# Local attention with two tiles per round instead of one

## The reference, cut to what matters

```python
bl = 128; nb = L // bl; G = L // 16          # L = 1024, H = 16 heads of 64
q = einsum('bld,dhk->blhk', x, Wq) / sqrt(64); k, v = ... Wk, Wv
side_k, side_v = (sum of x over 16 rows) @ Wk, Wv          # G = 64 rows
kb, vb = previous, own and next block of k, v              # 3 * 128 rows
logits = q_block @ concat(kb, side_k) + bias               # |distance| <= 127, else -1e9
m = max(logits.max(), 0)
probs = exp(logits - m) / (sum(exp(logits - m)) + exp(-m))
y = probs @ concat(vb, side_v)
x = x + einsum('blhk,hkd->bld', y, Wo)
```

## Time and profile before

| | us |
|---|---|
| median of three runs | 2113.58 |
| profiled execution | 2099.86 |
| its span (first to last instruction) | 2098.1 |
| PE matmul busy | 1908.6 (91%) |
| PE weight loads busy | 1372.2 (65%) |
| DVE busy | 1121.4 (53%) |
| ACT busy | 944.6 (45%) |
| POOL busy | 449.3 (21%) |

### The profile page before, as it was taken

One profiled execution on the slowest core, in us unless ns is written; L12 is line 12 of the kernel. 1 busy time (PEld: TensorE's weight loads), 2 busy tenths in 40 slices (PEclk: granted clock), 3 DMA queues, 4 the chain that ended last, 5 costly groups with the idle time before them and its releaser, 6 DMA issues.

```text
span 2098.1 us, 37599 instructions
## 1 busy us (share of the span) xinstructions
PE 1908.6 (91%) x15665; PEld 1372.2 (65%) x15665; DVE 1121.4 (53%) x2309; ACT 944.6 (45%) x1644; POOL 449.3 (21%) x502
## 2 busy tenths in 40 slices
PE   5888977995988949899999999999999999999998
PEld 3456965773656645667776776766777777777776
DVE  4474443016142126878887888854545543455544
ACT  2212022112242304778887888854454543445522
POOL 1352100004121033212121212112222222233313
PEclk8879567996998979999999999999999999999999
DMA  4000021112242339621100310000000000000001
GB/s 128 0 1 1 1 66 42 57 47 61 81 140 81 101 118 169 128 42 37 33 23 19 104 31 25 19 21 1 1 1 2 1 1 1 27 1 1 2 1 40
DMA packets 85194, 86.94 MB, mean 41 GB/s; under 512 B 34658, under 2 KB 70946, under 8 KB 84898
## 3 DMA queue, kind: packets, MB, share of 16 engines
q1 hardware_dynamic: 79154, 73.81, 13.2%
q0 software_dynamic: 3072, 8.39, 1.4%
q10 hardware_dynamic: 2800, 2.34, 0.4%
HBM read 65.65 MB, written 18.87 MB: 40 GB/s over the span
## 4 chain that ended last, share of the span: by engine, by line
PE 74%; DVE 18%; issue 3%; DMA 2%; POOL 1%; ACT 1%; SPq 0%; DVEq 0%; POOLq 0%
PE PS L1032 7%; DVE arena L1695 7%; PE PS L1024 7%; PE PS L1899 6%; PE PS L1883 6%; PE PS L1838 5%; PE PS L1528 5%; PE PS L1541 5%; PE PS L1873 5%; DVE arena L1700 4%; PE PS L519 3%; PE PS L1520 3%; PE PS L1843 3%; PE PS L1906 1%; PE PS L1933 1%
## 5 line engine op out<-in xcount | busy, mean ns | idle before, releaser
L1695 DVE CUSTOM_DVE_ANT_0 arena<-PS,arena 128x1024 f32<-128x1024 f32 x256 | 312.8, 1222 | 75.3 <-PE PS L1520 62.4
L1528 PE MATMUL PS<-arena 128*128 128x128 f32 x2048 | 281.8, 275 | 20.4 <-DVE arena L1700 20.2
L1619 ACT ACTIVATE arena<-arena 128x1024 f32<-128x1024 f32 x256 | 295.0, 1152 | 9.8 <-DVE arena L1695 9.8
L1528 PEld LDWEIGHTS PS<-arena 128*128 128x128 f32 x2048 | 241.4, 142 | 87.4 <-DVE arena L1700 34.8
L1980 ACT ACTIVATE arena<-arena 128x449 f32<-128x449 f32 (+1 forms) x256 | 162.5, 635 | 190.8 <-DVE arena L2014 190.8
L2069 POOL TENSOR_SCALAR arena<-arena 128x448 f32<-128x448 f32 (+1 forms) x256 | 154.3, 616 | 419.4 <-DVE arena L2005 419.4
L2014 DVE CUSTOM_DVE_ANT_0 arena<-PS,arena 128x448 f32<-128x448 f32 (+1 forms) x256 | 141.2, 590 | 138.9 <-PE PS L1874 138.0
L1615 ACT COPY arena<-PS 128x512 f32<-128x512 f32 x256 | 150.4, 588 | 102.9 <-PE PS L1528 94.7
L1700 DVE COPY arena<-PS 128x512 f32<-128x512 f32 x256 | 175.9, 687 | 1.2 <-PE PS L1528 1.2
L1024 PE MATMUL PS<-arena 128*128 128x512 f32 x384 | 170.2, 601 | 6.6 <-ACT arena L1123 6.6
L1032 PE MATMUL PS<-arena 128*128 128x256 f32 x768 | 172.2, 385 | 0.0
(11 more groups left out here) (279 smaller groups left out, 2657.0 us busy)
## 6 DMA issues: line engine op xcount, KB each, us to landing
arena<-in_L_ffn_W SPq DMA_DIRECT2D x16, 1024.0 KB, 6.6
arena<-prior SPq DMA_DIRECT2D x16, 512.0 KB, 4.0
parts<-arena SPq DMA_DIRECT2D x24, 256.0 KB, 5.4
arena<-parts SPq DMA_DIRECT2D x96, 64.0 KB, 2.9
arena<-parts SPq DMA_DIRECT2D x48, 128.0 KB, 10.5
ye<-arena SPq DMA_DIRECT2D x8, 512.0 KB, 3.5
prior<-arena SPq DMA_DIRECT2D x4, 1024.0 KB, 9.1
arena<-in_xT SPq DMA_DIRECT2D x2, 1024.0 KB, 8.0
```

The costliest lines, as they stand in the source:

```text
L1528: h = e.transpose(PS[:, i, P * j:P * j + P], Sb[z % 3][:, 512 * g + P * j:512 * g + P * j + P], ident)
L1619: e.activation(Sb[z % 3], Sb[z % 3], ACT.Exp, bias=mr[:, z % 4:z % 4 + 1], scale=-1.0).then_inc(s_exp, 1)
L1695: e.tensor_tensor_reduce(Sb[z % 3], ps, Ab[m % 2], 1.0, 3e38, ALU.add, ALU.min, mr[:, z % 4:z % 4 + 1]).then_inc(s_ttr, 1)
```

## The change

A round of every engine now takes two tiles, `z` and `z + 1` for even `z`. On PE:

- scores of `z` and `z + 1`; values of `z - 4` and `z - 3`; turn of `z - 2`, one piece of other work, turn of `z - 1`, another piece.
- The other work is listed by `between(z)`: chunks 0 and 1 in the first pair of a unit, 2 and 3 in the second, 4 in the third, 5 in the fourth. Projections come second in the third and fourth pairs (tiles 68, 70, 76, 78, 84, 86, 92 and 94).
- Values run two tiles behind the turn (one before).
- Scores have four banks (0 to 3), turned weights banks 4 and 5, values one bank (6), chunks and projections still bank 7. `Pb` has eight buffers. `Sb`, `Se` and `Pt` stay as they are.

ACT: `expo` of both tiles, then turn, chunk, turn, chunk. DVE: `biased` of both tiles, `recip(z)`, eviction of values, `recip(z + 1)`, then turn, work, turn, work. POOL's list stays.

```diff
-    Pb = [arena.up(512) for _ in range(6)]
+    Pb = [arena.up(512) for _ in range(8)]
...
-    N_ZERO = 13
-
-    def projected(z):
-        return (z - 66) // 2 if 65 < z < 82 and z % 2 == 0 else None
+    N_ZERO = 15
+    PRO = {z: t for t, z in enumerate(z for z in range(68, NZ, 2) if z % 8 in (4, 6))}
+    YB, CB = 6, 7
+    def between(z):
+        u, todo = z // 8 + 1, {0: (0, 1), 2: (2, 3), 4: (4,), 6: (5,)}[z % 8]
+        work = [(u, c) for c in todo] if u < NU else []
+        return work + ([("o", PRO[z])] if z in PRO and PRO[z] < TB_ else [])
...
         def scores(z):
-            w.wait_ge(*of(u).emptied((u, 5)))
+            w.wait_ge(*of(u).emptied((u, 1)))
...
-                w.wait_ge(s_ttr, x - 2)
+                w.wait_ge(s_ttr, x - 3)
...
         def values(z):
-            if t % 4 == 0:
-                w.wait_ge(s_y, n - 1)
+            w.wait_ge(*of(u).emptied((u, 5)))
+            w.wait_ge(s_y, n)
...
-        for z in range(NZ + 2):
-            if z < NZ:
-                scores(z)
-            if projected(z) is not None:
-                t = projected(z)
-                w.wait_ge(*ring.free(("o", t)))
-                project(0, t, ring.bank(("o", t))).then_inc(ring.sem, 1)
-            if 2 <= z:
-                values(z - 2)
-            if 1 <= z <= NZ:
-                turn(z - 1)
-            if z // 8 + 1 < NU and z % 8 < 6:
-                chunk(z // 8 + 1, z % 8)
+        for z in range(0, NZ + 4, 2):
+            for y in (z, z + 1):
+                if y < NZ:
+                    scores(y)
+            for y in (z - 4, z - 3):
+                if y >= 0:
+                    values(y)
+            work = between(z) if z < NZ else []
+            for y in (z - 2, z - 1):
+                if 0 <= y < NZ:
+                    turn(y)
+                if work:
+                    key = work.pop(0)
+                    if key[0] == "o":
+                        w.wait_ge(*ring.free(key))
+                        project(0, key[1], ring.bank(key)).then_inc(ring.sem, 1)
+                    else:
+                        chunk(*key)
...
     def act(e, w, own):
         def expo(z):
-                w.wait_ge(s_tf, x - 5)
+                w.wait_ge(s_tf, x - 7)
...
+        for z in range(0, NZ + 2, 2):
+            for y in (z, z + 1):
+                if y < NZ:
+                    expo(y)
+            work = between(z) if z < NZ else []
+            for y in (z - 2, z - 1):
+                if y >= 0:
+                    turn(y)
+                key = work.pop(0) if work else ("o",)
+                if key[0] != "o" and chunk_by(key[1]) == "act":
+                    chunk_out(e, w, *key)
...
     def dve(e, w, own):
+        for z in range(0, NZ + 4, 2):
+            for y in (z, z + 1):
+                if y < NZ:
+                    biased(y)
             if z < NZ:
-                biased(z)
...
+                recip(z)
+            for y in (z - 4, z - 3):
+                if y >= 0:
+                    values(y)
+            if z < NZ:
+                recip(z + 1)
+            work = between(z) if z < NZ else []
+            for y in (z - 2, z - 1):
+                if 0 <= y < NZ:
+                    turn(y)
+                if work:
+                    key = work.pop(0)
+                    if key[0] == "o":
+                        project(key[1])
+                    elif chunk_by(key[1]) == "dve":
+                        chunk_out(e, w, *key)
```

More of the change, by code:

```diff
@@ L1797, in phase_f @@
         first.plan(s, "dve" if s[0] == "sk" else "act")
-    for z in range(NZ):
-        if projected(z) is not None:
-            ring.plan(("o", projected(z)), "dve")
-        if z // 8 + 1 < NU and z % 8 < 6:
-            ring.plan((z // 8 + 1, z % 8), chunk_by(z % 8))
+    for z in range(0, NZ, 2):
+        for key in between(z):
+            ring.plan(key, "dve" if key[0] == "o" else chunk_by(key[1]))
     def f_steps(w):
@@ L1870, in scores @@
                 x, rows = 2 * z + d, slice(64 * d, 64 * d + 64)
-                w.wait_ge(s_ttr, x - 2)
+                w.wait_ge(s_ttr, x - 3)
                 q_ = q5[r][rows, P * t:P * t + P]
-                e.matmul(PS[:, x % 3, 0:nk], q_, k5[r][rows, P * k0:P * k1], start=True, stop=True)
-                e.matmul(PS[:, x % 3, nk:nk + 64], q_, sk[rows, u % 8, u // 8, :], start=True, stop=True).then_inc(s_sc, 1)
+                e.matmul(PS[:, x % 4, 0:nk], q_, k5[r][rows, P * k0:P * k1], start=True, stop=True)
+                e.matmul(PS[:, x % 4, nk:nk + 64], q_, sk[rows, u % 8, u // 8, :], start=True, stop=True).then_inc(s_sc, 1)
         def turn(z):
@@ L1882, in turn @@
                 for j in range(nj):
-                    h = e.transpose(PS[:, 3 + d, P * j:P * j + P], Pb[x % 6][:, P * j:P * j + P], ident)
+                    h = e.transpose(PS[:, 4 + d, P * j:P * j + P], Pb[x % 8][:, P * j:P * j + P], ident)
                 h.then_inc(s_tf, 1)
@@ L1898, in values @@
                     wt = v5[r][:, P * (k0 + j):P * (k0 + j) + P][:, c] if j < nj - 1 else sv[u // 8][:, u % 8, c]
-                    h = e.matmul(PS[c, 5 + n % 2, P * (t % 4):P * (t % 4) + P], wt, Pt[(2 * z + d) % 4][:, P * j:P * j + P], start=j == 0, stop=j == nj - 1)
+                    h = e.matmul(PS[c, YB, P * (t % 4):P * (t % 4) + P], wt, Pt[(2 * z + d) % 4][:, P * j:P * j + P], start=j == 0, stop=j == nj - 1)
             h.then_inc(s_val, 1)
@@ L1977, in expo @@
                 w.wait_ge(s_ttr, x + 1)
-                w.wait_ge(s_tf, x - 5)
+                w.wait_ge(s_tf, x - 7)
                 w.wait_ge(s_norm, 2 * z - 6)
-                e.activation(Pb[x % 6][:, 0:wd + 1], sbt[:, 0:wd + 1], ACT.Exp, bias=mr[:, g:g + 1], scale=-1.0, accum_out=sm[:, g:g + 1]).then_inc(s_exp, 1)
+                e.activation(Pb[x % 8][:, 0:wd + 1], sbt[:, 0:wd + 1], ACT.Exp, bias=mr[:, g:g + 1], scale=-1.0, accum_out=sm[:, g:g + 1]).then_inc(s_exp, 1)
         def turn(z):
@@ L1985, in turn @@
             w.wait_ge(s_val, z - 1)
-            e.copy(Pt[2 * z % 4][:, 0:n], PS[:, 3, 0:n]).then_inc(s_tc[0], 1)
+            e.copy(Pt[2 * z % 4][:, 0:n], PS[:, 4, 0:n]).then_inc(s_tc[0], 1)
         for c in (0, 1, 4, 5):
@@ L2013, in biased @@
                 w.wait_ge(s_sc, x + 1)
-                e.tensor_tensor_reduce(sbt[:, 0:wd], PS[:, x % 3, 0:wd], bnd, 1.0, 0.0, ALU.add, ALU.min, mr[:, g:g + 1]).then_inc(s_ttr, 1)
+                e.tensor_tensor_reduce(sbt[:, 0:wd], PS[:, x % 4, 0:wd], bnd, 1.0, 0.0, ALU.add, ALU.min, mr[:, g:g + 1]).then_inc(s_ttr, 1)
         def turn(z):
@@ L2019, in turn @@
             w.wait_ge(s_val, z - 1)
-            e.tensor_copy(Pt[(2 * z + 1) % 4][:, 0:n], PS[:, 4, 0:n]).then_inc(s_tc[1], 1)
+            e.tensor_copy(Pt[(2 * z + 1) % 4][:, 0:n], PS[:, 5, 0:n]).then_inc(s_tc[1], 1)
         def values(z):
@@ L2025, in values @@
                 w.wait_ge(s_val, z + 1)
-                e.tensor_copy(yT[u // 8][:, u % 8, 512 * (n % 2):512 * (n % 2) + 512], PS[:, 5 + n % 2, :]).then_inc(s_y, 1)
+                e.tensor_copy(yT[u // 8][:, u % 8, 512 * (n % 2):512 * (n % 2) + 512], PS[:, YB, :]).then_inc(s_y, 1)
         def project(t):
@@ L2041, in dve @@
             side_out(e, w, s)
-        for z in range(NZ + 2):
-            if 1 <= z <= NZ:
-                recip(z - 1)
+        for z in range(0, NZ + 4, 2):
+            for y in (z, z + 1):
+                if y < NZ:
+                    biased(y)
             if z < NZ:
-                biased(z)
[L2047 to L2054, removed]
+                recip(z)
[14 more added lines that the diff above has]
+                        chunk_out(e, w, *key)
     def pool(e, w, own):
@@ L2068, in pool @@
                 x, g = 2 * z + d, 2 * (z % 4) + d
-                e.tensor_scalar(Pb[x % 6][:, 0:wd], Pb[x % 6][:, 0:wd], sm[:, g:g + 1], 1.0, ALU.mult, ALU.mult).then_inc(s_norm, 1)
+                e.tensor_scalar(Pb[x % 8][:, 0:wd], Pb[x % 8][:, 0:wd], sm[:, g:g + 1], 1.0, ALU.mult, ALU.mult).then_inc(s_norm, 1)
     return sp, pe, act, dve, pool
```

## The result

| | before | after |
|---|---|---|
| median of the runs, us | 2113.21 (4 runs, 2109.4 to 2113.95) | 2087.95 (4 runs, 2078.43 to 2092.28) |
| ratio, 95% interval | | 0.9887 (0.9869 to 0.9905) |
| span of the profiled execution | 2098.1 | 2076.6 |
| the changed stage in it | 565.70 | 543.94 |
| what stands ahead of it | 1429.17 | 1429.51 |

The kernel is 25.3 us faster by the medians, 21.5 us by the two profiled spans, and 21.8 us of that is in the changed stage; everything else is the same within 0.4 us. The forecast was 2087.6 with a range of 2076 to 2101.

What follows compares the result with a forecast made beforehand. PE was taken as the bound, busy 561.34 of the stage's 565.70 us. Terms -32 - 4 - 2 + 7 + 2.4 + 2.1 + 0.5 = -26 us, applied to the median 2113.6, gave 2087.6 us; range 2076 to 2101.

Steps and rivals of the forecast that it cites:

- Two tiles per round: On PE, one set of shape-change borders per pair of tiles instead of two: 32 us gained, bounds 20 and 38.
- rival A: PE's scores keep their 0.27 us gap because it is the weights' time: gain only 14 us, 2099.6; chance 0.14.
- the 0.09 kept inside the scores: Per pair on PE, 0.09 us kept for loading the next tile's 128-column weights behind 64-column score records; bounds 0 and 0.27.
- its variant: On PE, a transpose after a chunk pays an entry of its own: 0.15 x 64 = 10 us, 2097.
- Values two tiles behind the turn: On PE, values no longer wait for the copy of freshly turned weights on tiles without a chunk before: 4 us gained.
- Projections: On PE, projections placed after a turn, between full-array work: 8 x 0.23 = 2 us gained; later next-stage loads cost nothing.
- One chunk bank: PE waits for the single chunk PSUM bank before second chunks: about 0.45 us a unit, 7 us lost; bounds 0 and 15.
- Order on ACT and DVE: Four score tiles' work precedes turned-weight copies: no cost in rounds with chunks, 0.6 us x 4 = 2.4 us lost in the last unit.
- Start, last unit and end together: PE waits for copies at the stage's edges: 2.1 us in the first round, 2.4 in the last unit, 0.5 at the end.
- Rival C: Turned weights copied too late on ACT, PE waits 0.6 to 0.65 us in 60 rounds: net +12, 2125.6; chance 0.07.
- Rival D: PE's borders are semaphore latencies paid behind any wait, not shape changes, so nothing changes in effect; chance 0.02.
- rival B: Late chunk copies on ACT and DVE make PE's second chunks wait: 26 us more, 2113, no change; chance 0.05.

Runs made afterwards that it cites:

- experiment 7: Changed kernel with the scores' second matmul over 128 columns of side keys instead of 64, except in the last unit: stage 550.22 us, one run 2095.85 us.
- experiment 3: Kernel before, one tile per round, with values a tile later, six turned-weight buffers and projections a round later: stage 562.99 us, ratio to before 0.9983.
- experiment 5: Changed kernel with a unit's chunks reordered (2; 0 and 3; 1 and 4; 5) and projections in first and fourth pairs: stage 539.64 us, median 2083.30 us.
- experiment 2: Changed kernel with the second tile's values after the first turn and chunk, DVE's eviction not moved: stage 587.58 us, ratio to before 1.0108.
- experiment 1: Changed kernel with PE alternating scores, values, scores, values in a round instead of both scores, then both values: stage 561.10 us, ratio to before 0.9979.
- experiment 6: The changed kernel itself, unaltered, run again: stage 543.94 us, beginning at 1440.90 us; median 2090.22 us, ratio to before 0.9898.

## Why the prediction was right, and by which steps

The total came within 0.4 us of the median. The parts show that some of this was luck.

- *Two tiles per round: right in mechanism, too large by a fifth.* The pair was to save 0.50 us. Measured: the scores of two tiles take 1.93 us (1606.42 to 1608.35) against 2 x 1.02; values 1.69 against 0.81 + 1.03 for the same records; a chunk between two turns 1.72 (1625.59 to 1627.31) against 1.81 ahead of scores; the second tile's turns no longer pay 0.06. That is 0.11 + 0.15 + 0.09 + 0.06 = 0.41, x 64 = 26 instead of 32 us, which is as far from the 0.50 of the forecast as from rival A's 0.32. The term mis-sized is the 0.09 kept inside the scores: it is about 0.16 (2 x 0.27 less the 0.11 saved leaves 0.43 for the pair, 0.16 above one tile's 0.27). Of it 0.11 went when the side-key records were made longer (experiment 7), which fits rival A's mechanism, weights that short records can't hide; 0.05 is not explained. Rival A had the whole at 0.27; the distance from the first to the second scores is 0.91, under the 1.0 that was to show it, and its variant, an entry paid by a transpose after a chunk, is excluded by the 1.78 from 1610.97 to 1612.75, of which 1.75 stream.
- *Values two tiles behind the turn:* 4 us predicted. Measured alone it is 2.7, with two longer turns a unit in it that the kernel after does not have (experiment 3). In the kernel after, the values of every pair start 0.31 us after the last score group starts, whether a chunk stood before or not, so the 4 us (29 x 0.14) are gone as predicted.
- *Projections:* a projection now adds 3.54 us (3.63 from 1711.33 to 1714.96, less the 0.09 that the turns' end costs anyway), 3.67 before: 1 us in all instead of 2. The loads of the next stage were issued at 1845.31, 48 us later than before; the prediction had some 60. POOL needed them at 1859.8, and waited for nothing.

The rows of the kernel after for this: the projection on PE.

```profile
1711.33 3.70 PE L1913 MATMUL PS<-arena 128*128 128x256 f32 x16
1714.96 0.92 PE L1880 MATMUL PS<-arena 64*128 64x384 f32 x4
```

SP's first issue for the next stage:

```profile
1845.31 0.38 SPq L2170 DMA_DIRECT2D arena<-in_L_ffn_W_r  x1
```

POOL's addition that needs it (durations min/median/max in ns, first and last start):

```profile
L2332 POOL TENSOR_TENSOR arena<-arena x8: 1088/1090/1097, 1859.8 to 2016.3; 128x512 f32<-128x512 f32 x8
```

- *One chunk bank:* 0.49 us a unit measured, 7.3 in all, against 7. The split between waiting and exposed loads was right as well (experiment 5).
- *Order on ACT and DVE:* no wait for a turned head's bank in the rounds with a chunk, as predicted, but for the second round: of ACT's 128 copies of turned heads PE waited for six only, one at the start and five at the end. PE's timeline of the first two rounds:

```profile
1431.20 1.98 PE L1845 MATMUL PS<-arena 128*128 128x512 f32 x4
1433.94 1.98 PE L1845 MATMUL PS<-arena 128*128 128x512 f32 x4 [0.76 <-ACT arena L1960]
...
1438.50 1.88 PE L1845 MATMUL PS<-arena 128*128 128x512 f32 x4
1440.78 1.09 PE L1890 MATMUL PS<-arena 128*128 128x128 f32 x8 [0.40 <-ACT arena L1998]
```

  and of a round of the last unit:

```profile
1946.08 1.09 PE L1890 MATMUL PS<-arena 128*128 128x128 f32 x8
1947.41 1.09 PE L1890 MATMUL PS<-arena 128*128 128x128 f32 x6 [0.24 <-ACT arena L1998]
```

  The first chunk pair cost 1.0 us of waiting (2.74 from 1431.20 to 1433.94, of which 1.72 is work) against 2.1 predicted, plus 0.6 before the second turn, which the prediction had left out. The second turn of this round of the last unit waits 0.40 us (1.33 from start to start, of which 0.93 is work) where 0.6 was predicted; the five such waits are of 0.4 to 0.6 us, and there are five and not four.
- *Start, last unit and end together:* predicted 2.1 + 2.4 + 0.5 = 5.0. The first unit took 28.69 us (1429.51 to 1458.20) instead of 31.44, and the last one with the end of the stage 31.00 (1942.45 to 1973.45) instead of 28.84: 0.6 less together. At the steady gain, 1.47 for the first (34.03 less 32.56) and 4 x 0.41 + 0.28 = 1.9 for the last, which has no chunks, it would have been 3.4 less, so the three cost 2.8. The end did not lose the 0.5: before its last two values PE has no wait any more (the earlier trace rows had 0.87 and 0.74).
- *Rival C* needed lateness of over 1.15 us on ACT. It did not occur in the changed kernel, but experiment 2 made its twin on DVE by leaving one instruction in an old place, and it cost 34 us: more than the pairing brings. So a copy that stands too far back on a half-idle engine can cost this much, and the change avoids it by its order; at 1.1 us a time it was dearer than the 0.6 that C had.
- Rival D, that the borders are not shape changes, is excluded by experiment 1; rival B, a bound by the chunk bank, by the 0.49 us a unit of experiment 5.

On the trace's scale the sum should have been -21.8, and was -26; the run's median moved by 25.3, with an interval of 20 to 28. The forecast's agreement with the median to 0.4 us is therefore no proof of its terms: the pair was 6 us too good and the projections 1, while start, last unit and end were 2 too bad. The other 3.5 us, between -21.8 and the median's -25.3, are within what executions of one kernel differ by ahead of the stage (experiment 6). With the measured terms the sum is -26 - 4 - 1 + 7 + 2.8 = -21; 1 us to the stage's 21.8 is not assigned.

The Trainium skill (TensorEngine Tiling, Key Properties) says that a change of tiling mode drains the array and a change of tile doesn't. The trace agrees on the first half as far as a price can show it: three changes a tile cost 0.59 us before, and two more a round cost 0.27 (experiment 1). On the second it adds that within the same mode the scores of two tiles still lost 0.16 us, of which 0.11 fits weight loads.

## What to carry to other kernels

When PE is "busy" all the time, measure start to start against what the records stream in: the difference at the borders between array shapes, here 0.59 us in 4.79, is the most that grouping work of one shape can save; two tiles together saved 0.41 of it. After reordering the bounding engine, walk through the order of every half-idle engine that feeds it: one instruction in front of a copy that was due cost more than the whole gain. Look for the single-bank ring behind a new order, too: which piece of work stands between its two uses, and who empties it, decided 4 us here.

## What was not expected

- The changed stage repeats to 0.01 us between executions (543.94 twice), while the code ahead of it took 11.4 us more in the one (up to 13 over all kernels), at a granted clock of 0.83 in the first 200 us against 0.86 in the other. As far as these two profiles show, a change in a late stage can be judged from a profile to a tenth of a microsecond, and by run times only to some 4 us.
- Widening a 64-column matmul to 128 columns on 64 rows cost only half of the time that the further columns stream in, which fits loads of its weights that took longer than its 64 columns.
- Moving chunks away from a wait gave back the wait, but only a part of what stood behind it: a chunk whose bank is free just in time still took 0.07 us more (1.88 against 1.81).
- Reaching some turns 0.1 to 0.2 us sooner made PE meet POOL's normalization, and took back more than half of what the later values gave in experiment 3.
